# A Mamba-2 mixer between two LoRA feed-forward layers: mixer steps taken two at a time, transposes and gates in two shared banks

## The reference

```
proj = layernorm(x) @ in_proj_w.T                # gate 8192, x 8192, B 1024, C 1024, dt 128
xBC  = silu(conv4(x, B, C) + conv_b)             # causal, four taps, per channel
for each of 8 groups (16 heads of 64 channels), chunks of 128 tokens:
    Y = ((C . B) * exp(decay between tokens), lower triangle) @ (x * dt) + x * D
yg = Y * silu(gate)
out = (yg / rms of yg over the group's 1024 channels) * norm_w @ out_proj_w.T
```

## Time and profile before

| | us |
|---|---|
| median of 3 runs | 1623.67 (1623.44 to 1627.81) |
| profiled execution | 1627.01 |
| its span | 1625.2 |
| PE busy | 1564.3 (96%) |
| DVE busy | 1228.0 (76%) |
| POOL busy | 1052.0 (65%) |
| ACT busy | 1002.3 (62%) |

### The profile page before, as it was taken

One profiled execution on the slowest core, in us unless ns is written; L12 is line 12 of the kernel. 1 busy time (PEld: TensorE's weight loads), 2 busy tenths in 40 slices (PEclk: granted clock), 3 DMA queues, 4 the chain that ended last, 5 costly groups with the idle time before them and its releaser, 6 DMA issues. The chain is left out here.

```text
span 1625.2 us, 25474 instructions
## 1 busy us (share of the span) xinstructions
PE 1564.3 (96%) x8296; PEld 1226.0 (75%) x8296; DVE 1228.0 (76%) x1689; ACT 1002.3 (62%) x2122; POOL 1052.0 (65%) x790
## 2 busy tenths in 40 slices
PE   6979999999999999999999999999999999999979
PEld 4657777777777777777777777777777777777757
DVE  6688877787778877887688877887688877887565
ACT  4357765666666665666666665666666665666431
POOL 2017874788757874788657874787657874787620
PEclk9899999999999999999999999999999999999989
DMA  3033321323222221222212321223222221322011
GB/s 118 1 103 103 107 91 59 92 91 92 78 72 92 92 92 59 91 92 92 78 72 92 92 91 59 92 92 92 78 75 88 92 92 59 98 86 84 20 40 53
DMA packets 73658, 131.65 MB, mean 81 GB/s; under 512 B 10944, under 2 KB 10944, under 8 KB 73280
## 3 DMA queue, kind: packets, MB, share of 16 engines
q1 hardware_dynamic: 73536, 130.09, 24.3%
HBM read 127.44 MB, written 2.62 MB: 80 GB/s over the span
## 5 line engine op out<-in xcount | busy, mean ns | idle before, releaser
L892 DVE SCALAR_TENSOR_TENSOR mx_acc<-bank,mx_cw,mx_acc 128x510 f32<-128x510 f32 (+2 forms) x480 | 358.3, 746 | 160.8 <-ACT mx_acc L877 149.5
L159 PE MATMUL bank<-h_hi,mx_w_hi 128*128 128x512 f32 x1152 | 465.6, 404 | 4.4 <-DVE mx_acc L892 2.3
L161 PE MATMUL bank<-h_hi,mx_w_lo 128*128 128x512 f32 x1152 | 453.1, 393 | 0.0
L160 PE MATMUL bank<-h_lo,mx_w_hi 128*128 128x512 f32 x1152 | 450.2, 391 | 0.0
L1108 ACT ACTIVATE mx_mix<-mx_csb,mx_gncs 128x256 f32<-128x256 f32 x512 | 218.9, 499 | 284.3 <-PE bank L1478 281.3
L1033 POOL TENSOR_TENSOR mx_y<-mx_y,mx_sg 128x512 f32<-128x512 f32 x128 | 338.4, 2644 | 59.7 <-DVE mx_y L1280 51.7
L839 POOL TENSOR_TENSOR mx_w_lo<-mx_w_raw,mx_w_hi 128x512 fp32r<-128x512 f32 x144 | 187.4, 1302 | 111.0 <-ACT mx_w_hi L834 111.0
L161 PEld LDWEIGHTS bank<-h_hi,mx_w_lo 128*128 128x128 f32 x1152 | 216.9, 188 | 48.5
L159 PEld LDWEIGHTS bank<-h_hi,mx_w_hi 128*128 128x128 f32 x1152 | 217.3, 189 | 47.8 <-issue 6.5
L160 PEld LDWEIGHTS bank<-h_lo,mx_w_hi 128*128 128x128 f32 x1152 | 217.7, 189 | 41.5
L1262 DVE TENSOR_TENSOR mx_mix<-mx_mix,mx_cbt 128x1536 f32<-128x1536 f32 x128 | 224.5, 1754 | 0.0
(11 more groups left out here) (163 smaller groups left out, 2203.7 us busy)
## 6 DMA issues: line engine op xcount, KB each, us to landing
mx_csb<-cs_rows SPq DMA_DIRECT2D x128, 512.0 KB, 4.0
mx_w_raw<-in_w_in SPq DMA_DIRECT2D x144, 256.0 KB, 4.0
mx_wo_raw<-in_w_out SPq DMA_DIRECT2D x64, 256.0 KB, 4.2
res<-in_x SPq DMA_DIRECT2D x8, 256.0 KB, 5.0
f_base_raw<-in_base_wt SPq DMA_DIRECT2D x2, 1024.0 KB, 6.1
out<-res SPq DMA_DIRECT2D x8, 256.0 KB, 2.0
f_a_raw<-in_lora_a SPq DMA_DIRECT2D x2, 256.0 KB, 3.8
f_lb_raw<-in_lora_b SPq DMA_DIRECT2D x2, 256.0 KB, 6.2
```

The source lines that it names most:

```text
L159: nc.tensor.matmul(out, w_hi, x_hi, start=first, stop=False)
L160: nc.tensor.matmul(out, w_hi, x_lo, start=False, stop=False)
L161: return nc.tensor.matmul(out, w_lo, x_hi, start=False, stop=last)
L892: self.nc.vector.scalar_tensor_tensor(dst, src[:, :, 0:SEQ - k], self.cw[:, c, TAPS - 1 - k:TAPS - k], dst, ALU.mult, ALU.add).then_inc(s[ ...
```

## The change

Two steps, 2j and 2j + 1, are taken together, as pair j. PE now does in a pair: both transposes, two projections, both gates, both output tiles, both mixings. In pair 0 the transposes come after the projections. The units projected in pair j are 2j + 6 and 2j + 7 (those of the next pair), in the last pair units 0 and 1 of the next group; the tail has units 2 to 5. The bank of transposes and the bank of gates become two banks that each serve one step of the pair for both: the transposed x of a step, then, once DVE has read it (`xd`), its gate. The next pair's transposes wait for the gate's silu (`sg`) in turn. The sums over channels use the first of them.

The other engines' lists are put in the order of pairs too, and GpSimd's `mask_diagonals` is split in two, `mask_first` (ahead, for the next pair) and `mask_second`. The copy of a group's decays (`gncs`, `decay_constants`) is gone: ACT reads the whole array `m.ncs`, with the head's number. SP's loop over the groups is written out. The arithmetic and the number of the other instructions stay.

Banks and the lists that the new order is made of:

```diff
-        G_BANK, T_BANK, Y_BANK, O_BANK = m.bank[2], m.bank[3], m.bank[4:6], m.bank[6:8]
+        TG_BANK, Y_BANK, O_BANK = (m.bank[3], m.bank[2]), m.bank[4:6], m.bank[6:8]
+        SUM_BANK = TG_BANK[0]
...
+        def units_of(g, j):
+
+            if j < PAIRS - 1:
+                return [(g, 2 * j + 6), (g, 2 * j + 7)]
+            return [(g + 1, 0), (g + 1, 1)] if g + 1 < NG else []
+
+        def weights_split_in(g, j):
+
+            if j == 0:
+                return [WPG * g + 5, WPG * g + 6, WPG * g + 7]
+            return [WPG * g + 2 * j + 6, WPG * g + 2 * j + 7] if j < PAIRS - 1 else [WPG * g + 2 * j + 6]
...
```

SyncE:

```diff
+            def pair(g, j):
+                load_w(WPG * g + 2 * j + 7)
+                next_cs(g, 2 * j + 2)
+                load_w(WPG * g + 2 * j + 8)
+                next_cs(g, 2 * j + 3)
+                if j + 1 < XT:
+                    load_wo(g, j + 1)
+                if j == 5 and g + 1 < NG:
+                    ip.load_constants(sp, g + 1)
```

GpSimd:

```diff
+            def pair(g, j):
+                steps, before = (2 * j, 2 * j + 1), (2 * j - 2, 2 * j - 1)
+                if j == 0:
+                    remainder_w(WPG * g + 5)
+                else:
+                    for st in steps:
+                        mask_second(g, st)
+                    for st in before:
+                        gate_y(g, st)
+                    for p in steps:
+                        if has_tile(g, p):
+                            split_tile(g, p)
+                mask_ahead(g, 2 * j + 2)
+                if j >= 2:
+                    for st in before:
+                        sum_squares(g, st)
+                mask_ahead(g, 2 * j + 3)
+                for n in weights_split_in(g, j):
+                    if n % WPG != 5:
+                        remainder_w(n)
+
+            def tail(g, more):
                 if more:
-                    ip.remainder_w(pool, g + 1, 3)
-
-            for g in range(NG):
-                group(g, g + 1 < NG)
-            for p in range(1, XT):
-                split_tile(NG, p)
+                    for st in range(2):
+                        mask_second(g + 1, st)
+                gate_y(g, STEPS - 2)
+                gate_y(g, STEPS - 1)
+                if more:
+                    remainder_w(WPG * (g + 1) + 3)
+                split_tile(g + 1, 0)
+                sum_squares(g, STEPS - 2)
+                sum_squares(g, STEPS - 1)
+                if more:
+                    remainder_w(WPG * (g + 1) + 4)
+                split_tile(g + 1, 1)
```

ScalarE:

```diff
+            def pair(g, j):
+                units, splits = units_of(g, j), weights_split_in(g, j)
+                a, b = 2 * j, 2 * j + 1
+                if j == 0:
+                    round_w(splits.pop(0))
+                else:
+                    decay_from_first(g, a)
+                    decay_from_second(g, a)
+                    for p in (a, b):
+                        if has_tile(g, p):
+                            round_tile(g, p)
+                if j == PAIRS - 1 and units:
+                    act.wait_ge(s["const"], 1 + 4 * (g + 1) + 2)
+                if units:
+                    evacuate(*units[0])
+                if j > 0:
+                    decay_from_first(g, b)
+                if units:
+                    evacuate(*units[1])
+                if j > 0:
+                    decay_from_second(g, b)
+                    square(g, a - 2)
+                    square(g, a - 1)
+                if j == 0 and g > 0:
+                    root(g - 1)
+                if units:
+                    tanh_conv(*units[0])
+                tanh_gate(g, a)
+                if units:
+                    tanh_conv(*units[1])
+                tanh_gate(g, b)
+                for n in splits:
+                    round_w(n)
+                split_wo(g, j)
+                for p in (a, b):
+                    if p >= XT:
+                        keep_first_quad(g, p)
...
             def tail(g, more):
-                keep_first_quad(g, STEPS - 1)
-                round_tile(g + 1, 0)
                 if more:
-                    evacuate(g + 1, 1)
-                    square(g, STEPS - 1)
-                    ip.round_w(act, g + 1, 2)
-                    tanh_conv(g + 1, 1)
+                    decay_from_first(g + 1, 0)
+                    decay_from_second(g + 1, 0)
                     evacuate(g + 1, 2)
+                    square(g, STEPS - 2)
+                    round_w(WPG * (g + 1) + 3)
                     evacuate(g + 1, 3)
                     tanh_conv(g + 1, 2)
+                    round_tile(g + 1, 0)
+                    square(g, STEPS - 1)
+                    round_w(WPG * (g + 1) + 4)
                     tanh_conv(g + 1, 3)
                     evacuate(g + 1, 4)
-                    ip.round_w(act, g + 1, 3)
+                    decay_from_first(g + 1, 1)
+                    evacuate(g + 1, 5)
                     tanh_conv(g + 1, 4)
-                    root(g)
+                    decay_from_second(g + 1, 1)
+                    round_tile(g + 1, 1)
+                    tanh_conv(g + 1, 5)
```

VectorE:

```diff
+            def pair(g, j):
+                units = units_of(g, j)
+                a, b = 2 * j, 2 * j + 1
+                if j > 0:
+                    skip_y(g, a - 2)
+                    skip_y(g, a - 1)
+                scale_x(g, a)
+                scale_x(g, b)
+                make_mix(g, a)
+                if j == 0:
+                    make_mix(g, b)
+                if j == PAIRS - 1 and units:
+                    ip.conv_constants(dve, g + 1)
+                for u in units:
+                    taps(*u)
+                if j > 0:
+                    make_mix(g, b)
+                if units:
+                    silu_conv(*units[0])
+                silu_gate(g, a)
+                if units:
+                    silu_conv(*units[1])
+                silu_gate(g, b)
+                split_wo(g, j)
+                if j == 0 and g > 0:
+                    inverse(g - 1)
+                for n in (a, b):
+                    if n < XT and has_tile(g, n):
+                        add_quads(g, n)
+                        add_group(g, n)
             def tail(g, more):
+                skip_y(g, STEPS - 2)
                 skip_y(g, STEPS - 1)
                 if more:
                     head_constants(g + 1)
-                    taps(g + 1, 1)
-                    silu_conv(g + 1, 1)
                     taps(g + 1, 2)
+                    taps(g + 1, 3)
                     silu_conv(g + 1, 2)
-                    taps(g + 1, 3)
-                    keep_bc(g + 1, 0)
-                    mean_square(g)
                     silu_conv(g + 1, 3)
                     taps(g + 1, 4)
+                    taps(g + 1, 5)
+                    mean_square(g)
+                    silu_conv(g + 1, 4)
+                    silu_conv(g + 1, 5)
+                    keep_bc(g + 1, 0)
                     keep_bc(g + 1, 1)
```

TensorE:

```diff
-                pe.wait_ge(s["xd"], 1 + STEPS * g + st)
+                if not (first(g) and st < 2):
+                    pe.wait_ge(s["sg"], 1 + STEPS * g + st - 1)
                 for t in range(2 * HB):
-                    last = nc.tensor.transpose(T_BANK[:, t * P:(t + 1) * P],
+                    last = nc.tensor.transpose(TG_BANK[st % 2][:, t * P:(t + 1) * P],
                                                acc[:, st % 4, t // 2, t % 2 * CH:(t % 2 + 1) * CH], m.ident[:, :])
                 last.then_inc(s["xt"], 1)
...
                 w, hf = 3 + 2 * (st // 2), st % 2
                 pe.wait_ge(s["wlo"], 1 + WPG * g + w + 1)
-                pe.wait_ge(s["sg"], 1 + STEPS * g + st)
+                pe.wait_ge(s["xd"], 1 + STEPS * g + st + 1)
                 at = slice(hf * HALF, (hf + 1) * HALF)
                 for k in range(KT):
-                    last = three_pass(nc, G_BANK[:, :], w_hi[:, w % 3, k, :], w_lo[:, w % 3, k, :],
+                    last = three_pass(nc, TG_BANK[st % 2][:, :], w_hi[:, w % 3, k, :], w_lo[:, w % 3, k, :],
                                       m.h_hi[:, k, at], m.h_lo[:, k, at], k == 0, k == KT - 1)
...
+            def pair(g, j):
+                steps = (2 * j, 2 * j + 1)
+                if j > 0:
+                    for st in steps:
+                        transpose_x(g, st)
+                for u in units_of(g, j):
+                    ip.project(pe, *u)
+                if j == 0:
+                    for st in steps:
+                        transpose_x(g, st)
+                for st in steps:
                     project_gate(g, st)
-                    if has_tile(g, st):
-                        project_out(g, st)
+                for p in steps:
+                    if has_tile(g, p):
+                        project_out(g, p)
+                for st in steps:
                     mix_tokens(g, st)
             def tail(g, more):
                 if more:
-                    ip.project(pe, g + 1, 1)
```

(33 more changed lines are left out.)

189 lines of the change are left out of this document (58 added, 131 removed).

## The result

The changed kernel takes 1588.46 us (median of 4, 1584.46 to 1590.12) beside 1625.51 us before: a ratio of 0.9768, interval 0.9742 to 0.9794. A second set gave 0.9762 (0.9739 to 0.9784). The forecast was 1594 us, within 1587 to 1612. The profiled execution took 1590.12 us, its span is 1588.3 (before 1627.01 and 1625.2).

What follows compares the result with a forecast made beforehand. PE was taken to bound the mixer, through idle places and time between matmuls. Savings of 18 + 9.3 + 3 - 0.7 = 29.6 us took the profiled 1627.0 to 1597.4, the median to 1594 us; range 1587 to 1612.

Steps and rivals of the forecast that it cites:

- Part 1: PE, mixings and transposes two in a row: 0.30 us saved per merged block, 60 blocks, 18 us; a pair takes 20.27.
- The rest in time for a pair: Mid-group: the other engines and the new wait for `xd` keep up with PE's 20.27 us a pair, costed at nothing.
- The margin I gave for DVE: Pairs with additions: DVE's busy time plus in-order waits comes to 18.9 us, under PE's 20.27.
- Part 2: Seven group boundaries: 1.88 us of PE stall goes, 0.55 comes at pair 0's gate; 9.3 us saved in all.
- the forecast's 0.55: Pair 0: PE loses 0.55 us after both transposes, as the gate waits for `scale_x`.
- The margins of 0.8 us in the tail: Group's tail: sums over channels, both ahead of the second C.B, have about 0.8 us in hand before POOL has them.
- Part 3: First group's first half and the two ends: 3 us saved (0 to 5), 0.7 lost at the last pair's gate.
- the pair of 15.2 us: First group's first half: DVE, 13.95 us busy plus waits of about 1.2, sets the pair; three pairs save 0.9 each.
- The last pair's gate: Last pair, no projections between transposes and gate: the gate waits for a `skip_y` and a `scale_x`, 0.7 us lost.
- Rivals 1 and 2: Change of form isn't the price, 1612 us, 10%; the group boundary stays a stall, 1603 to 1606 us, 15%.
- Rival 3: Pairs with additions in groups 1 to 7: POOL's products hold DVE off and it becomes the bound; 1635 us, 8%.
- Rival 4: Something costed at nothing adds a new wait of up to 0.2 us in each pair; 1607 us, 7%.

Runs made afterwards that it cites:

- the transposes between: Changed kernel with both of pair 0's transposes moved between its two projections, so the second projection runs while DVE scales x; 1581.59 us, ratio 0.9735.

## Why the prediction was right

**Part 1.** Right in mechanism, and tested from both sides. Mis-sized: 0.41 us for each merged block instead of 0.30, which makes 24.6 instead of 18 us. My list priced the entry, the first records, the exit, and the transposes with the first matmul behind them. It left out that a train of 512-column matmuls doesn't start at its steady pace: before, gaps of 0.231 to 0.236 were frequent in the first dozen matmuls behind the transposes and settled at 0.227; after, they end with the sixth. One long train instead of two saves about 0.1 us of it. (From the starts in both traces: 36 matmuls in a row took 8.10 us from first to last start, 72 take 16.24. Two of the one and one of the other, less one gap of 0.23, differ by 0.19; 0.09 is the longer first gap, which my list had; 0.10 is pace.) I took 0.228 for all.

**The rest in time for a pair.** Right in outcome: no wait for `xd` in pairs 1 to 6, no idle time in the middle of a group. The margin I gave for DVE (18.9 of 20.27) was wrong in kind: DVE is busy for 19.6, because POOL's products now run beside its mixes and silus, and a pair still bears 1.9 us more. I had added up instructions of the old lengths; that DVE would be in time in spite of longer ones, I had not worked out.

**Part 2.** Right: 1.88 went and 0.63 came, counted from start to start like the forecast's 0.55 (0.44 of it as idle time). That makes 1.25; the boundary gained about 1.5 against 1.33 forecast, and I can't place the 0.25. The margins of 0.8 us in the tail held.

**Part 3.** The number is luck in part. To step 8 the transposes come 2.7 us earlier (forecast 3), but 1.8 of that was there before the mixer began. From the mixer's first matmul to step 2 it took 48.61 us before and 48.85 after (47.69 to 49.15 in six profiles of the changed kernel and its variants): the first pair came out even, as forecast, though with one projection more done in it, which is 2.7 us of PE work that the last group then saves. The step that failed is the pair of 15.2 us: pairs 1 to 3 took 15.6, 16.24 and 16.34, together 48.2 against 49.3 before, so 1.1 was saved and not 2.7. The second transposes wait 0.57 to 1.06 us for the gate's silu, behind a silu that POOL holds off, and in pairs 2 and 3 the mixings take 3.16 us instead of 2.76, since DVE's product for the second (2.37 us long instead of 1.75) ends only when PE wants it. DVE was busy for 16.10 of 16.24 us, where I had 13.95 and waits of 1.2. The last pair's gate cost 0.52 (forecast 0.7), and the pause at the end stayed, 3.43 us.

**Rivals.** Rivals 1 and 2 didn't come, the first by experiment. Rival 3's lock is there, but as a wait that DVE can bear in the middle of a group. Rival 4, a new wait in each pair, didn't come either: a pair takes 20.16 us without idle time.

**What remained of the difference to the forecast.** The two profiled executions differ by 36.9 us, the forecast's sum was 29.6: part 1's size gives +6.6, the boundaries +1.2, the last pair's gate +0.2, the first group about -0.7 (2.3 instead of 3). The two stretches outside the mixer are scatter, +1.8 ahead and -1.8 behind; the one behind took 89.2 us at a mean clock of 0.88 in the changed kernel's profile and 84.5 at 0.95 in that of the transposes between, with the same 320 matmuls:

```profile
1499.10:1588.30 89.20, 76.58 (x320) 58.46 (x320) 49.26 (x117) 22.23 (x39) 18.14 (x15) 0.88 0.12 42
```

```profile
1493.10:1577.60 84.50, 71.55 (x320) 54.41 (x320) 49.23 (x117) 22.14 (x39) 18.13 (x15) 0.95 0.12 44
```

## What to carry to other kernels

When PE is busy all the time, read its starts, not its busy time: 0.41 us for every second block of another column form was 1.5% of this kernel (24.6 us in 60 pairs), and ordering blocks of the same column form next to each other took it away without touching the work. What stands between a group's last product and its next first one should be work whose operands are long there. An engine that shows 97% busy need not be full: waits inside its instructions count as work, and adding work tells how much.

## What the runs showed of the hardware that I had not expected

- An additional block of 128*64 matmuls among 128*128 ones costs 0.36 us (20.52 against 20.16 a pair); an additional block of fp32 transposes among fp32r matmuls 0.03.
- 512-column matmuls behind such blocks start up to 0.236 us apart at first, for about ten matmuls in the kernel before and five in the changed one, before they settle at 0.227. I have no cause for it.
- DVE and POOL hold each other off (a silu of 0.68 us took 1.77 beside a POOL product), and the waiting counts as busy: 1.9 us of reductions a pair raised DVE's busy time by 0.2.
- Two short pauses with four transposes between them (0.79 and 1.02 to 1.05 us) stood at seven boundaries. At four of them a stretch followed in which the granted clock averaged 0.61 to 0.63; at three it stayed at 1.00.
